# Graph attention on one core: in the steps, TensorE's semaphores raised by a drain instead of by the last matmul

## The reference

```python
def _gat_layer(h_in, W, a_s, a_d, b, src, dst, n):
    h = (h_in @ W).reshape(n, Hh, Cc)
    alpha_s = jnp.sum(h * a_s, axis=-1)
    alpha_d = jnp.sum(h * a_d, axis=-1)
    e = jax.nn.leaky_relu(alpha_s[src] + alpha_d[dst], 0.2)
    m = jax.lax.stop_gradient(jax.ops.segment_max(e, dst, num_segments=n))
    ex = jnp.exp(e - m[dst])
    alpha = ex / jax.ops.segment_sum(ex, dst, num_segments=n)[dst]
    out = jax.ops.segment_sum(h[src] * alpha[:, :, None], dst, num_segments=n)
    return out.reshape(n, Hh * Cc) + b

h = jnp.maximum(_layernorm(x, axis=-1), 0.0)
h = gelu(_gat_layer(h, W0, ...)); h = gelu(_gat_layer(h, W1, ...))
return x + h
```

## Time and profile before

| what | value |
|---|---|
| median of 3 runs | 5397.24 us (5339.36 to 5411.88) |
| profiled execution, its own time | 5438.12 us |
| its span, first to last instruction | 5436.3 us |
| granted TensorE clock, mean | 0.72 of full speed |
| busy: PE / PE weight loads / DVE / ACT / POOL | 52% / 35% / 64% / 41% / 62% |

### The profile page before, as it was taken

How to read it: one execution, slowest core, us unless ns; L and a number is a source line. 1 busy time by engine, 2 the same in 40 slices (tenths; PEclk the granted TensorE clock), 3 DMA queues, 4 the chain that set the end, 5 groups by cost and what they waited for, 6 DMA issues and landing times. The chain is left out here.

```text
span 5436.3 us, 62905 instructions
## 1 busy us (share of the span) xinstructions
PE 2832.3 (52%) x9790; PEld 1912.7 (35%) x9790; DVE 3472.3 (64%) x12389; ACT 2231.9 (41%) x6943; POOL 3358.4 (62%) x3189
## 2 busy tenths in 40 slices
PE   6455545555555655555544554455444455454554
PEld 5333333333333433333333333333333233333333
DVE  5467657666666766666655666666666566676666
ACT  4244434434444444444433444344433344343434
POOL 3466656666666666666646666666666566666663
PEclk9777777777777777777767767777767677676777
DMA  6444434443344444444434444444444444444442
GB/s 210 122 121 115 119 107 123 115 114 110 109 119 118 124 118 116 117 113 114 113 91 120 125 129 132 122 129 129 127 125 124 121 129 132 125 132 124 128 131 83
DMA packets 342319, 662.83 MB, mean 122 GB/s; under 512 B 99106, under 2 KB 211530, under 8 KB 341914
## 3 DMA queue, kind: packets, MB, share of 16 engines
q0 software_dynamic: 151056, 429.17, 30.0%
q1 hardware_dynamic: 128952, 172.16, 10.7%
q10 hardware_dynamic: 62018, 59.05, 3.2%
HBM read 597.44 MB, written 62.65 MB: 121 GB/s over the span
## 5 line engine op out<-in xcount | busy, mean ns | idle before, releaser
L501 POOL DMA_INDIRECT rows_all<-table,edge x3136 | 3317.3, 1058 | 2006.8 <-issue 1481.6
L1138 PE MATMUL bank<-rows_all,onehot 128*128 128x264 f32 x6272 | 1967.0, 468 | 61.6 <-remote 38.8
L1138 PEld LDWEIGHTS bank<-rows_all,onehot 128*128 128x128 f32 x6272 | 1415.1, 236 | 426.1 <-issue 144.7
L1112 PE MATMUL bank<-onehotT,logit_p 128*128 128x448 bf16 x896 | 369.5, 566 | 1321.7 <-issue 867.3
L572 ACT ACTIVATE rows_all<-rows_all 128x64 f32<-128x64 f32 x3584 | 876.7, 333 | 10.2 <-issue 10.1
L867 DVE TENSOR_TENSOR rows_all<-rows_all 128x768 f32<-128x768 f32 (+1 forms) x672 | 694.6, 1034 | 0.0
L1112 PEld LDWEIGHTS bank<-onehotT,logit_p 128*128 128x128 bf16 x896 | 96.8, 127 | 1533.9 <-issue 1331.8
L1148 PE MATMUL bank<-total,heir 128*128 128x264 f32 x448 | 192.1, 518 | 750.8 <-DVE heir L990 370.0
L585 ACT ACTIVATE share<-node_d 128x8 f32<-128x8 f32 x224 | 46.7, 209 | 1192.7 <-DVE node_d L950 834.5
L608 ACT ACT_TABLE_LOAD x224 | 287.4, 1283 | 548.9 <-issue 438.9
L889 DVE TENSOR_TENSOR onehot<-iota_f,dloc 128x1792 f32<-128x1792 f32 x224 | 453.9, 2026 | 0.0
(11 more groups left out here) (165 smaller groups left out, 3642.6 us busy)
## 6 DMA issues: line engine op xcount, KB each, us to landing
dst_b<-dst_row SPq DMA_DIRECT2D x224, 448.0 KB
rows_all<-table,edge POOLq DMA_INDIRECT x3136
self_row<-table SPq DMA_DIRECT2D x224, 132.0 KB
table<-row ACTq DMA_DIRECT2D x113, 132.0 KB
x_row<-in_x_dram SPq DMA_DIRECT2D x112, 128.0 KB
out_dram<-y_out ACTq DMA_DIRECT2D x112, 128.0 KB
act_pad<-act_o ACTq DMA_DIRECT2D x112, 128.0 KB
table<-row ACTq DMA_DIRECT2D x24, 528.0 KB, 3.7
```

What stands on the lines that cost most here:

```text
L501: nc.gpsimd.indirect_dma_start(out=G[u][:, j, :], out_offset=None, in_=table[L][0:N, :], in_offset=bass.IndirectOffsetOnAxis(ap=index[:, j ...
L1112: last = nc.tensor.matmul(bank[0][:, 0:SLOTS * SQ], logit_p[:, q * P:(q + 1) * P], of[:, q], start=(q == 0), stop=(q == QUADS - 1))
L1138: last = nc.tensor.matmul(bank[3 + t.half][:, 0:ROW], onehot[t.half][:, j, :], G[t.u][:, j, :], start=(j == 0), stop=(j == SLOTS - 1))
```

## The change

At seven places of the steps the increment is taken off the last matmul and put on a drain that follows it in TensorE's stream. The dense stage is left as it is: there the matmuls still raise their semaphores. Nothing else changes; all waits, matmuls and tiles stay, and so do the streams of the other engines. Five of the drains stand in each of the 224 steps, the two of `transpose_act` and `next_rows` only in the steps of layer 0. From L1106 on, line numbers of the changed kernel are one to three higher.

```diff
                 for q in range(QUADS):
-                    last = nc.tensor.matmul(bank[0][:, 0:SLOTS * SQ], logit_p[:, q * P:(q + 1) * P], of[:, q], start=(q == 0), stop=(q == QUADS - 1))
-                last.then_inc(s["ad_done"], 1)
+                    nc.tensor.matmul(bank[0][:, 0:SLOTS * SQ], logit_p[:, q * P:(q + 1) * P], of[:, q], start=(q == 0), stop=(q == QUADS - 1))
+                nc.tensor.drain().then_inc(s["ad_done"], 1)
...
-                nc.tensor.transpose(bank[1][0:H, P:2 * P], behind[:, :, 0], ident[:]).then_inc(s["rowT_done"], 1)
+                nc.tensor.transpose(bank[1][0:H, P:2 * P], behind[:, :, 0], ident[:])
+                nc.tensor.drain().then_inc(s["rowT_done"], 1)
...
-                nc.tensor.transpose(bank[2][:, H:2 * H], carry[:, 1, :], ident[0:H, 0:H]).then_inc(s["carryT_done"], 1)
+                nc.tensor.transpose(bank[2][:, H:2 * H], carry[:, 1, :], ident[0:H, 0:H])
+                nc.tensor.drain().then_inc(s["carryT_done"], 1)
...
                 if part == DVE_PARTS:
-                    last.then_inc(s["sum_done"], 1)
+                    nc.tensor.drain().then_inc(s["sum_done"], 1)
...
-                nc.tensor.matmul(bank[5][:, 0:ROW], heir[:], total[:].rearrange("p h c -> p (h c)"), start=True, stop=True
-                                 ).then_inc(s["old_done"], 1)
+                nc.tensor.matmul(bank[5][:, 0:ROW], heir[:], total[:].rearrange("p h c -> p (h c)"), start=True, stop=True)
+                nc.tensor.drain().then_inc(s["old_done"], 1)
...
-                    last.then_inc(s["actT_done"], 1)
+                    nc.tensor.drain().then_inc(s["actT_done"], 1)
...
-                    last.then_inc(s["row_done"], 1)
+                    nc.tensor.drain().then_inc(s["row_done"], 1)
```

More of the change, by code:

```diff
@@ L1137, in sum_up @@
                 for j in range(t0, t1):
-                    last = nc.tensor.matmul(bank[3 + t.half][:, 0:ROW], onehot[t.half][:, j, :], G[t.u][:, j, :],
+                    nc.tensor.matmul(bank[3 + t.half][:, 0:ROW], onehot[t.half][:, j, :], G[t.u][:, j, :],
                                             start=(j == 0), stop=(j == SLOTS - 1))
                 if part == DVE_PARTS:
-                    last.then_inc(s["sum_done"], 1)
+                    nc.tensor.drain().then_inc(s["sum_done"], 1)
             def hand_over(t):
@@ L1155, in transpose_act @@
                     for j in range(KC):
-                        last = nc.tensor.transpose(bank[6][:, j * P:(j + 1) * P], act_o[t.half][:, j * P:(j + 1) * P], ident[:])
-                    last.then_inc(s["actT_done"], 1)
+                        nc.tensor.transpose(bank[6][:, j * P:(j + 1) * P], act_o[t.half][:, j * P:(j + 1) * P], ident[:])
+                    nc.tensor.drain().then_inc(s["actT_done"], 1)
             def next_rows(t):
@@ L1163, in next_rows @@
                     for j in range(KC):
-                        last = nc.tensor.matmul(bank[7][:, 0:ROW], act_oT[:, j, :], w_ext[:, 1, j, :],
+                        nc.tensor.matmul(bank[7][:, 0:ROW], act_oT[:, j, :], w_ext[:, 1, j, :],
                                                 start=(j == 0), stop=(j == KC - 1))
-                    last.then_inc(s["row_done"], 1)
+                    nc.tensor.drain().then_inc(s["row_done"], 1)
             def pe_body(earlier, before, now, after):
```

## The result

The changed kernel takes 5577.87 us (median of 4 runs, 5567.18 to 5602.5), the kernel before 5402.28 us (4 runs, 5339.36 to 5411.88): 1.0354 times as long (the ratio of the means; that of the medians is 1.0325, 176 us), 95% interval 1.0305 to 1.0402. The forecast, 4880 us, was wrong in its direction; 5577.87 lies in its range only because that reached to the first rival, at 5620 us. The profiled execution took 5602.5 us against 5438.1 before.

A forecast was written before the change was run, and what follows sets the result against it. VectorE's chain, waiting for late matmul increments, was taken to bound the kernel: 5438.1 - 675 + 78 + 75 = 4916 us, times 0.9925, gives 4880 us. The forecast's own range was 4760 to 5100 us, with rivals 4760 to 5640.

The forecast's parts named there:

- the first rival: TensorE's drains are held as the increments were and block its later work: slower, 5620 us, chance 0.31.
- The reading at the top: Matmul increments are at times held many microseconds after the array's work; VectorE's chain, which sets the step, pays.
- Term (a): VectorE's waits at L903 and L968 go if a drain's increment is not held: -675 us of 708.7.
- The row on which I leaned: VectorE's L950 ends at 2040.36 and ScalarE's L585, waiting for its increment, starts at 2040.39: semaphores take increments at once.
- The rule of the Trainium skill: A drain waits until the engine is fully idle, so one behind a held matmul would be held too.
- the two rivals that rest on it: Drain held and TensorE blocked, 5620 us, chance 0.31; drain held without effect, 5400 to 5475 us, chance 0.19.
- Term (b): Each TensorE drain exposes about 0.35 us, about one a step on VectorE's chain: +78 us.
- the bound of 470 us: Upper bound on the drains' cost: all 1344 at about 0.35 us each, none hidden by TensorE's idle time.
- The prediction's sign for (b): The drain cost is wrong if the sum's matmuls (L1138) idle over 300 us in steps with nothing late.
- Term (c): Same gathers in less time: the 376.4 us of waits at L881 and L854 grow by a fifth, +75 us.
- The floor of the gathers: GpSimd's gathers with their gaps take 4258 us, some 4500 with the time around the loop; not yet binding.
- The loads: SyncE's edge-record loads delay gathers in shorter steps, L873 waits, half the gain is lost: 5140 us, chance 0.12.

## Why the prediction was wrong

**The reading at the top was half right.** Increments of TensorE's matmuls do come late on that chip: where nothing is late the unchanged kernel takes 4654 to 4657 us instead of 5402, and VectorE's idle time before L903 and L968 is gone. But so is that before L844, L854, L856, L858 and L881, 623.4 us against 26. VectorE's own results were late too, and the prediction took the two groups for different things. It is a comparison of chips, which may differ in more than this.

**Term (a), -675 us, is the step that failed.** It held that a drain's increment would not be held in the same way. It is: 9.16 us at L1131, up to 28.5 before L968, 826.2 us for the 708.7 in sum. The row on which I leaned, an increment of VectorE's own that came at once in the earlier trace rows, was one case and no rule: in the same trace L854 waits for L852 alone, with 45 waits put down to "remote" of 141.8 us in all, the longest 4.9. The 141.8 us stand in the earlier trace rows. For TensorE the records of the drains show more than a late message: the engine itself stands. The rule of the Trainium skill that the prediction set against it said so, and the two rivals that rest on it should have had more than 0.31 and 0.19. The sign for it that the prediction named, many microseconds of idle time before TensorE's next matmul, is what the profile shows.

**Term (b), +78 us, was too small by more than a factor of two.** It measured 173 us without gathers and 185 with half of them. The drain behind `logits_to_edges` costs 68 of it, 0.30 us a step, close to the 0.35 assumed. Wrong was "about one drain a step": in layer 0 two stand in a row ahead of `ends_to_rows`, and the second (with that of `next_rows`) costs 0.83 us a step more, over half of it with a slower clock in the first part of the sum, of which the prediction has no term. The drains of rowT, carryT, the sum and `hand_over`, the other 896 of the 1344, cost nothing by themselves and 12 us on top of the rest, so the bound of 470 us was rightly not taken. The prediction's sign for (b), over 300 us before the sum's matmuls in quiet steps, was no good one: without gathers these have 123.5 us, and the price shows before L901.

**Term (c), +75 us,** rested on (a) and was not tested as such. The two groups that it wanted to grow, 376.4 us at L881 and L854, have 274.9; what grew is L844, which it did not name. The floor of the gathers that it named, about 4500 us, is real: on the quiet chips the kernel and its forms run at 4654 to 4674 us with 649 to 716 us of waits at L873. There a working (a) would have ended at that floor.

**The first rival** came nearest, 5620 against 5577.87 us: the drain is held and TensorE stands at it. Its working was not right, though. It took 129 us for work that starts late behind held drains and 78 for (b); the runs give 173 to 185 for (b) alone, and don't show what the held drains cost. Part of its nearness is luck. Its 0.5 us a step from which it decides were met by drains that are not held. The loads did not take over: L873 has 49.3 us before it. And the low end of the forecast's own range, 4760, lacks the factor 0.9925 (4727), which changes nothing here.

## What to carry to other kernels

A drain behind matmuls costs what stands behind it on TensorE before the next result that somebody waits for: with nothing in between it was free here, in a chain of short pieces it was 0.3 us, and 0.8 us for a second one, behind which the clock was lower. It does not make a late completion early; it makes TensorE wait for it too. Before taking late increments for those of one engine, look whether an engine waits long for its own results in the same trace. And before reading a wait as a property of the kernel, see it on a second chip: here the bound changed from late results to the gathers, and with it the price of the same edit from 3.5% to 0.3%.

## What was unexpected of the hardware

The same kernel takes 5402 and 5302 us on two chips and 4654, 4657 and 4656 on three others, each within 1.4% of itself. On a chip of the first kind VectorE waited up to 28.5 us at L968, for a matmul that was over by its modelled end, and up to 4.9 us at L854, for its own preceding instruction, while GpSimd issued 14 gathers a batch; with 7, on the other chip of that kind, 6.3 us and 0.7 were the longest in the kernel before. Two stops that put TensorE's next work back by 0.5 to 0.7 us went with a granted clock of 0.50 in a further 3.2 us in which TensorE was busy 3.14; over layer 0 it was 0.53 in that part for 0.65 without drains. And a drain placed directly behind the transposes that VectorE waits for did not delay VectorE measurably (3898.26 against 3905.24 us).
